# ELU in two ACT passes and one DVE pass, and a one-pass normalisation, in a linear-attention layer

## What is computed

```python
        qkv = x @ w_qkv + b_qkv
        ...
        q = jax.nn.elu(q) + 1.0
        k = jax.nn.elu(k) + 1.0
        kv = jnp.einsum('bhnd,bhne->bhde', k, v)
        out = jnp.einsum('bhnd,bhde->bhne', q, kv)
        z = 1.0 / (jnp.einsum('bhnd,bhd->bhn', q, k.sum(axis=2)) + 1e-08)
        out = out * z[..., None]
```

## Time and profile before

| | |
|---|---|
| device time, three runs | 1470.67, 1473.27, 1473.92 us (median 1473.27) |
| span of the profiled execution | 1432.3 us |
| device time of the profiled execution | not recorded by itself |
| the stage of the change | from 336 us (first transfers) to 492 us (last scatter) |
| busy: PE, DVE, ACT, POOL | 1099.4, 834.6, 544.6, 484.7 us |
| mean granted TensorE clock | 0.886 of full speed |

### The profile page before, as it was taken

One profiled execution on the slowest core, in us unless ns is written; L12 is line 12 of the kernel. 1 busy time (PEld: TensorE's weight loads), 2 busy tenths in 40 slices (PEclk: granted clock), 3 DMA queues, 4 the chain that ended last, 5 costly groups with the idle time before them and its releaser, 6 DMA issues.

```text
span 1432.3 us, 39482 instructions
## 1 busy us (share of the span) xinstructions
PE 1099.4 (77%) x16860; PEld 814.9 (57%) x16860; DVE 834.6 (58%) x2486; ACT 544.6 (38%) x919; POOL 484.7 (34%) x555
## 2 busy tenths in 40 slices
PE   5899938992766398376788888889888887762996
PEld 3677727992655266253455565656565564442885
DVE  6577744654877311525857768585858675733343
ACT  3223102221542132141456373737465553450442
POOL 3123331332767300424131324324231403022576
PEclk9999969996987599577899999999999999776998
DMA  9940033653200241211112021222121100103685
GB/s 375 397 180 18 19 112 105 198 160 114 89 15 23 62 95 47 66 51 52 50 45 61 12 69 52 56 58 63 51 62 48 46 22 11 53 20 102 150 212 112
DMA packets 89204, 126.46 MB, mean 88 GB/s; under 512 B 14914, under 2 KB 67396, under 8 KB 88612
## 3 DMA queue, kind: packets, MB, share of 16 engines
q1 hardware_dynamic: 72868, 107.79, 24.0%
q0 software_dynamic: 11936, 14.04, 4.4%
q10 hardware_dynamic: 4224, 2.10, 0.5%
HBM read 53.10 MB, written 44.83 MB: 68 GB/s over the span
## 4 chain that ended last, share of the span: by engine, by line
PE 26%; DVE 19%; ACT 8%; DMA 3%; POOL 3%; issue 3%; SPq 2%; POOLq 0%; DVEq 0%; ACTq 0%
DVE mx L1497 9%; ACT MW L1710 4%; PE ps L791 2%; PE ps L713 2%; PE ps L965 2%; PE ps L699 2%; PE ps L805 2%; DVE mx L1488 2%; PE ps L908 2%; PE ps L899 2%; PE ps L821 1%; PE ps L900 1%; DMA MW<-l_moe_dram 1%; DVE X L1028 1%; DVE bst L1000 1%
## 5 line engine op out<-in xcount | busy, mean ns | idle before, releaser
L1497 DVE TENSOR_REDUCE mx<-ps 128x2 f32<-128x1024 f32 (+3 forms) x176 | 188.5, 1120 | 33.2 <-PE ps L938 33.1
L1710 ACT ACTIVATE MW<-ps 128x1024 f32<-128x1024 f32 x160 | 154.6, 1028 | 74.9 <-PE ps L950 74.4
L1830 POOL DMA_INDIRECT xs<-xr,sidu x96 | 95.4, 994 | 141.9 <-DVE sidu L1158 104.2
L1773 POOL TENSOR_SCALAR rst<-bmv 128x4 f32<-128x4 f32 x64 | 15.6, 243 | 246.2 <-DVE bmv L1003 241.1
L713 PE MATMUL ps<-tmpA,MW 128*128 128x256 f32 x336 | 92.7, 392 | 6.9 <-DMA MW<-l_moe_dram 3.5
L965 PE MATMUL ps<-MW,Vp 128*16 128x128 f32 x2560 | 87.8, 279 | 3.6 <-ACT MW L1710 3.5
L531 PE MATMUL ps<-W,xr 128*128 128x128 f32 x192 | 38.3, 335 | 64.5 <-DVE xr L1013 35.3
L1858 POOL DMA_INDIRECT out_dram<-qf,toku x46 | 71.5, 1554 | 42.7 <-DVE toku L1320 34.5
L699 PE MATMUL ps<-MW 128*128 128x128 f32 x672 | 82.0, 275 | 3.0 <-DVE qf L1305 1.5
L699 PEld LDWEIGHTS ps<-MW 128*128 128x128 f32 x672 | 78.5, 192 | 3.4 <-issue 3.3
L938 PE MATMUL ps<-K,Q 64*128 64x512 bf16 (+3 forms) x512 | 62.8, 319 | 22.2 <-DVE mx L1497 15.3
(11 more groups left out here) (319 smaller groups left out, 2537.9 us busy)
## 6 DMA issues: line engine op xcount, KB each, us to landing
xs<-hb SPq DMA_DIRECT2D x66, 384.0 KB, 4.2
MW<-l_moe_dram SPq DMA_DIRECT2D x19, 768.0 KB, 5.5
MW<-l_moe_dram SPq DMA_DIRECT2D x23, 578.0 KB, 5.1
Q<-spl SPq DMA_DIRECT2D x48, 128.0 KB
K<-spl SPq DMA_DIRECT2D x48, 128.0 KB
Q<-spm SPq DMA_DIRECT2D x48, 128.0 KB
K<-spm SPq DMA_DIRECT2D x48, 128.0 KB
tmpA<-xs SPq DMA_DIRECT2D x42, 132.0 KB, 2.2
```

The source lines that it names most:

```text
L1497: V.tensor_reduce(out=mx[1][:, :, s0:s0 + ns, t], in_=p.rearrange("p (e n) -> p e n", e=2)[:, :, 0:ns * nk].rearrange("p e (s k) -> p e s ...
L1710: A.activation(P3[k % 2][:, 1024 * half:1024 * half + 1024], p, ACT.Exp).then_inc(drained[u], 1)
L1830: G.indirect_dma_start(out=xs[L], out_offset=bass.IndirectOffsetOnAxis(ap=sidu[:, 4 * b + t:4 * b + t + 1], axis=0), in_=src[:, t, 0:128 i ...
```

## The change

POOL no longer takes part in `l1_qe` and `l1_ke`, and neither does DVE. ACT writes Relu(-x), which is -min(x, 0), to `rr`, and then Exp of its negative in place. DVE's `l1_qf` and `l1_kf` become one operation, max(x, 0) + `rr`, in place over q or k. The due times of `l1_qe` and `l1_ke` on ACT change from 51.43 and 51.92 to 46.43 and 46.92. In `l1_o` one operation over all four tiles takes the place of four. Semaphores `q1_neg`, `k1_neg`, `q1_exp`, `k1_exp` take the place of `elu_min` and `elu_exp`.

```diff
--- before.py
+++ after.py
@@ -115,10 +115,10 @@
     ("l1a_y", dict(ACT=19.59, POOL=61.22)),
     ("l1a_n", dict(PE=52.57, ACT=31.47)),
     ("l1_q", dict(PE=66.51, ACT=45.57)),
-    ("l1_qe", dict(DVE=48.64, ACT=51.43, POOL=41.55)),
+    ("l1_qe", dict(ACT=46.43)),
     ("l1_kv", dict(PE=64.39, DVE=35.61)),
     ("l1_qf", dict(DVE=57.21)),
-    ("l1_ke", dict(DVE=43.88, ACT=51.92, POOL=44.94)),
+    ("l1_ke", dict(ACT=46.92)),
     ("l1_kf", dict(DVE=53.29)),
     ("l1_st", dict(PE=90.45, DVE=62.59)),
     ("l1_o", dict(PE=93.61, DVE=67.61)),
@@ -299,7 +299,7 @@
          "pv0", "pv1", "og_out0", "og_out1",
          "logits_on", "hot", "tsub", "texp", "slots", "scatter0", "scatter1", "y0_in", "y1_in", "mixed",
          "tab", "gx0", "gx1", "gx2", "gx3", "gw0", "gw1", "gw2", "gw3", "turned", "gT", "g_act", "g_down", "g_y", "g_tok",
-         "y_out0", "y_out1", "y_out2", "y_out3", "rope", "tanh", "padded", "elu_min", "elu_exp", "elu_max", "q1_in", "q1_on", "k1_on",
+         "y_out0", "y_out1", "y_out2", "y_out3", "rope", "tanh", "padded", "q1_neg", "k1_neg", "q1_exp", "k1_exp", "q1_in", "q1_on", "k1_on",
          "mx0", "mx1", "m_turn", "mT", "m_down", "m_out0", "m_out1", "m_y"]
         + [f"{n}{k}" for n in ("stats", "rstd", "xn_done") for k in range(4)]
         + [f"{n}{k}" for n in ("hi", "rest", "mid", "low", "max_hi", "max_mid", "max_low") for k in range(2)]
@@ -1355,16 +1355,10 @@
                     x_at[b] = (sem["mixed"], b + 1)
                 elif name == "l1a_s":
                     ln_stats((name, b))
-                elif name == "l1_qe":
-                    e.wait_ge(drained_of(("l1_q", b)), after(("l1_q", b)))
-                    if b > 0:
-                        e.wait_ge(sem["q1_on"], b)
-                    settled()
-                    own.end(V.tensor_scalar(out=kf[:, :], in0=q1[i], scalar1=0.0, scalar2=None, op0=ALU.max))
                 elif name == "l1_qf":
-                    e.wait_ge(sem["elu_exp"], 2 * b + 1)
-                    settled()
-                    V.tensor_tensor(out=q1[i], in0=rr[0][:, :], in1=kf[:, :], op=ALU.add).then_inc(sem["q1_on"], 1)
+                    e.wait_ge(sem["q1_exp"], b + 1)
+                    V.scalar_tensor_tensor(out=q1[i], in0=q1[i], scalar=0.0, in1=rr[0][:, :], op0=ALU.max,
+                                           op1=ALU.add).then_inc(sem["q1_on"], 1)
                 elif name == "l1_kv":
                     u, n, p = unit((name, b))
                     pv = p.rearrange("p (t n) -> p t n", t=4)
@@ -1375,15 +1369,9 @@
                     V.tensor_tensor(out=k1[i], in0=pv[:, :, 0:128], in1=bc(w("l1_bkv")[:, 0:128], 1, [128, 4, 128]), op=ALU.add)
                     V.tensor_tensor(out=l1v[i][:, :, 0:128], in0=pv[:, :, 128:256], in1=bc(w("l1_bkv")[:, 128:256], 1, [128, 4, 128]),
                                     op=ALU.add).then_inc(drained[u], 1)
-                elif name == "l1_ke":
-                    e.wait_ge(drained_of(("l1_kv", b)), after(("l1_kv", b)))
-                    if b > 0:
-                        e.wait_ge(sem["k1_on"], b)
-                    own.end(V.tensor_scalar(out=op_[0].rearrange("p g q -> p (g q)"), in0=kk, scalar1=0.0, scalar2=None, op0=ALU.max))
                 elif name == "l1_kf":
-                    e.wait_ge(sem["elu_exp"], 2 * b + 2)
-                    settled()
-                    V.tensor_tensor(out=kk, in0=rr[1][:, :], in1=op_[0].rearrange("p g q -> p (g q)"), op=ALU.add).then_inc(sem["k1_on"], 1)
+                    e.wait_ge(sem["k1_exp"], b + 1)
+                    V.scalar_tensor_tensor(out=kk, in0=kk, scalar=0.0, in1=rr[1][:, :], op0=ALU.max, op1=ALU.add).then_inc(sem["k1_on"], 1)
                 elif name == "l1_st":
                     u, n, p = unit((name, b))
                     if b > 3:
@@ -1404,10 +1392,8 @@
                     settled()
                     own.end(V.reciprocal(rd, rd))
                     settled()
-                    for t in range(4):
-                        m = V.tensor_tensor(out=tc4[:, t, :].rearrange("p (h e) -> p h e", h=H), in0=pv[:, t, 0:128].rearrange("p (h e) -> p h e", h=H),
-                                            in1=bc(rd[:, t, :], 2, [128, H, 8]), op=ALU.mult)
-                    m.then_inc(drained[u], 1)
+                    V.tensor_tensor(out=tc4[:, :, :].rearrange("p t (h e) -> p t h e", h=H), in0=pv[:, :, 0:128].rearrange("p t (h e) -> p t h e", h=H),
+                                    in1=bc(rd, 3, [128, 4, H, 8]), op=ALU.mult).then_inc(drained[u], 1)
                 elif name == "l1_pj":
                     x_at[b] = (sem["bias_done"], B + b + 1)
                     add_x4((name, b), b)
@@ -1635,8 +1621,13 @@
                     A.activation(q1[i], p[:, 0:512], ACT.Identity, bias=w("l1_bq")).then_inc(drained[u], 1)
                 elif name in ("l1_qe", "l1_ke"):
                     j = 0 if name == "l1_qe" else 1
-                    e.wait_ge(sem["elu_min"], 2 * b + j + 1)
-                    A.activation(rr[j][:, :], rr[j][:, :], ACT.Exp).then_inc(sem["elu_exp"], 1)
+                    src = q1[i] if j == 0 else k1[i].rearrange("p t d -> p (t d)")
+                    made = ("l1_q" if j == 0 else "l1_kv", b)
+                    e.wait_ge(drained_of(made), after(made))
+                    e.wait_ge(sem["q1_on" if j == 0 else "k1_on"], b)
+                    A.activation(rr[j][:, :], src, ACT.Relu, scale=-1.0).then_inc(sem["q1_neg" if j == 0 else "k1_neg"], 1)
+                    e.wait_ge(sem["q1_neg" if j == 0 else "k1_neg"], b + 1)
+                    A.activation(rr[j][:, :], rr[j][:, :], ACT.Exp, scale=-1.0).then_inc(sem["q1_exp" if j == 0 else "k1_exp"], 1)
                 elif name == "l1_tr":
                     u, n, p = unit((name, b))
                     if b > 0:
@@ -1872,15 +1863,6 @@
                     rstd((name, b))
                 elif name == "l1a_y":
                     add_bias(("l1a_n", b), "l1_bproj")
-                elif name == "l1_qe":
-                    e.wait_ge(drained_of(("l1_q", b)), after(("l1_q", b)))
-                    e.wait_ge(sem["q1_on"], b)
-                    G.tensor_scalar(out=rr[0][:, :], in0=q1[b % 4], scalar1=0.0, scalar2=None, op0=ALU.min).then_inc(sem["elu_min"], 1)
-                elif name == "l1_ke":
-                    e.wait_ge(drained_of(("l1_kv", b)), after(("l1_kv", b)))
-                    e.wait_ge(sem["k1_on"], b)
-                    G.tensor_scalar(out=rr[1][:, :], in0=k1[b % 4].rearrange("p t d -> p (t d)"), scalar1=0.0, scalar2=None,
-                                    op0=ALU.min).then_inc(sem["elu_min"], 1)
                 elif name == "l1t_x":
                     scatter(1, b)
             for k in range(2):
```

## The result

The changed kernel takes 1484.64 us in the median (11 runs, 1477.47 to 1490.01), the kernel before 1473.27 us (11 runs, 1467.06 to 1477.48) on the same chip: a ratio of 1.0078, interval 1.0059 to 1.0097. That is 11.4 us or 0.8% slower, where +6.0 us was forecast; the time lies inside the range of 1467 to 1488 us. The change is almost twice the forecast, and lies outside the 3 to 10 us that the forecast called its own mechanism.

A forecast was written before the change was run, and what follows sets the result against it. The prediction took a ring of handovers between engines in the linear-attention stage as the bound. Terms 3.0 + 3.5 + 0.8 + 3.5 - 3.3 - 1.3 - 0.2 gave +6.0 us: 1473.27 to 1479.3 us, range 1467 to 1488 us.

The forecast's parts named there:

- its own mechanism: Linear-attention stage: ACT's moved passes lengthen the handovers between engines, slower by 3 to 10 us, chance 0.49.
- The moved block ahead of `l1_tr`: On ACT, both Relu and Exp pairs now stand between XT and l1a_y, delaying l1_tr; about 2.4 us before next work.
- The wait for `l1_qf`: ACT's first Relu of a batch waits for DVE's l1_qf of the batch before, about 1 us in four or five batches.
- The length of the block: ACT from the end of l1_qf to l1_tr: 4.0 us with l1a_y; one Relu and Exp pair 1.30 us.
- DVE from `l1_kv` to the end of `l1_qf`: DVE's part of the four steps between batches 3 and 7, taken as 3.9, 5.4, 6.05 and 5.4 us.
- PE from `l1_pj` to the next `l1_kv`: PE's part of the four steps between batches 3 and 7, taken as 6.8, 6.8, 5.5 and 6.1 us.
- The clearly slower rival: PE's lower clock holds through l1_kv in each of four rounds, 7.2 us more: +13, 1486.5 us; chance 0.12.
- Before batch 3: Table load and first block ahead of l1a_y make l1_tr of batch 0 and l1_kv of batch 3 start 3.0 us later.
- After batch 7: From l1_kv of batch 7 to ACT's next normalisation: 16.2 us instead of 17.54, so -1.3 us.
- The relief of POOL and DVE: POOL loses 16 min passes, about 1.65 us each; DVE loses 16 clamps, those of l1_ke 0.42 to 0.83 us.
- the faster rival: ACT's block does not delay the handovers, leaving only POOL's and DVE's savings: -7.6 us, 1465.7 us; chance 0.19.
- The rule against Relu on ScalarE: Skill's rule that relu, max and min belong on VectorE; with the clamp there the sum would be about -0.5.

The follow-up runs named there:

- e1_late: Changed kernel with the due times of l1_qe and l1_ke on ACT put back, so both pairs stand behind l1_tr; ratio 0.9974 to the kernel before.
- e3_two_buffers: Changed kernel with two buffers for each rr, so a Relu waits for the addition of two batches earlier; ratio 1.0043 to the kernel before.
- e4_pool_min_fused: Kernel before with only DVE's maximum and addition fused, min staying on POOL and normalisation in four passes; ratio 0.9976 to the kernel before.
- e7_pool_min_norm: Kernel before with the fused DVE pass and one-pass normalisation, min staying on POOL, Exps at their old place; ratio 0.9980 to the kernel before.
- e8_pool_min_early: Kernel before with fused DVE pass, one-pass normalisation and Exps moved ahead of l1_tr, min staying on POOL; ratio 1.0101 to the kernel before.
- e9_both_behind_fn: Changed kernel with two rr buffers, both pairs behind l1_tr and the q pair also behind l1f_n's XT copy; ratio 0.9977 to the kernel before.
- e11_late_fill: Changed kernel with two rr buffers, both pairs behind l1_tr, and one unread matmul filling PE's pause there; ratio 0.9947 to the kernel before.
- e6_after_again: Changed kernel, unaltered, run on the other sort of chip; ratio 1.0055 to the kernel before on that chip.

## Why the prediction was right, and where its size was off

- **The moved block ahead of `l1_tr`: right, and shown.** It was named as the part that counts, and `e1_late` takes it back alone.
- **The wait for `l1_qf`: right.** Forecast about 1 us in four or five batches; measured 0.81 to 1.69 us in six, batch 6 among them, which the prediction had thought free of it. `e3_two_buffers` puts it at 4.9 us of the four steps and 3.2 us of the stage.
- **The length of the block: right.** Forecast 4.0 us from the first Relu to `l1_tr`, measured 3.92, and 2.38 where forecast was 2.45 for batch 6; a pair 1.30, measured 0.66 + 0.63. The Trainium skill, page "ScalarE: Activation LUTs", section "What ACT_TABLE_LOAD costs", gives 186 ns + 0.833 ns per element for an ACTIVATE with immediate scale and bias: 0.61 us here, an estimate by that page; the rows agree with 0.61 to 0.64. No table load was added.
- **DVE from `l1_kv` to the end of `l1_qf`: right in sum, two rounds off.** Forecast 3.9, 5.4, 6.05, 5.4; to the Relu's start they are 4.9, 5.5, 5.5 and 5.5. The 1.0 us in the first is the fused pass of 1.58 us in place of 0.68 (below). The fusion had been costed at nothing for each pass, which holds for 15 of the 16. With the block, `l1_kv` to `l1_pj` was forecast at 37.6 us over the four and is 37.9.
- **PE from `l1_pj` to the next `l1_kv`: the term that was mis-sized.** The sum took 6.8, 6.8, 5.5 and 6.1; measured are 9.57, 6.69, 6.87 and 7.70, together 30.8 instead of 25.2. That is 5.6 us, nearly all of the 6.0 by which the steps (68.78) exceed the forecast's (62.8). I had taken two stretches of the kernel before, 6.8 and 5.5, and their mean as if they held for all rounds, though its own four are 6.8, 9.5, 5.5 and 7.4, together 29.1: the 3.76 us of `l1_kv` in the earlier trace rows stand in the 9.5. So 3.9 of the 5.6 us were there before the change and had been dropped from the sum without a reason, and 1.7 were added by it. The clearly slower rival had the mechanism, the lower clock after PE's pause, as an addition of 7.2 us; what was wrong was to hold it for an alternative to the forecast, since both act in the same round. It had the lower level hold through `l1_kv` in all four rounds; it did in one (3.53 us, 1.97 in the others). Its +13 us is nearer to the measured +11.4 than the forecast's +6.0, and it had been given 0.12.
- **Before batch 3:** +3.0 forecast; `l1_kv` of 3 starts 37.4 us into the stage instead of 35.4, so +2.0.
- **After batch 7:** 16.2 forecast, 15.56 measured (467.66 to 452.10, the start of the next normalisation on ACT), where it was 17.54 before. To the end of the stage only 0.9 us of that gain is left, where 1.3 + 0.2 had been forecast.
- **The relief of POOL and DVE: smaller than in the faster rival.** That rival had 7.6 us. Where the passes stand behind `l1_tr` the stage is shorter than before by 3.8 (`e1_late`), 4.6 (`e4_pool_min_fused`) and 1.4 us (`e7_pool_min_norm`), and none of the three ratios excludes no change. The old step 6 to 7, of which 3.3 us were to go with POOL's passes, gave back 1.7.
- **The rule against Relu on ScalarE** (the Trainium skill, "ScalarE: Activation LUTs", "Rules for kernel authors"): a clamp on VectorE in the same place was not run. `e1_late` shows that the passes cost nothing measurable on ACT where ACT is waiting anyway, and `e8_pool_min_early` that having them elsewhere, there on POOL, doesn't help where the place is wrong.
- **The sentence on 41.0 us around the span was wrong**, as the first section shows. It changed no term, since the sum was one of differences inside the stage.

## What to carry to other kernels

Where each engine works a fixed list in order, cost a moved instruction by who waits for the instruction behind it, not by its length: 2.5 us of work a batch, and the wait that came with it, ahead of the copy that PE waits for cost some 15 us over eight batches, and the same work behind it nothing that could be measured. Add up every round of the kernel before, the slow ones too, before taking a good one for all. When a change lengthens a pause of TensorE, take the matmuls right behind the pause at the lower clock unless a row of this very round says otherwise; here a few matmuls whose result nobody reads kept it high. Before adding a difference to a median, see that the span and the median are of the same chip.

## What the hardware showed that I had not expected

**The clock after a pause.** The granted clock has two levels, 1.2 and 2.4 GHz, and `l1_pj` shows which one holds: 1.16 us at the upper, about 2.08 at the lower. After pauses of 6.03, 5.52, 5.52 and 3.98 us (changed kernel) it took 2.07 or 2.08 each time. After the shorter ones it goes either way: 1.16 after 1.43 and 1.97 us in the kernel before and after 3.35 us in `e7_pool_min_norm`, but 2.08 after 1.83 us in `e9_both_behind_fn`, and after only 0.68 us in the kernel before (429.88 us):

```profile
412.90 2.08 PE L771 MATMUL ps<-W,oT 128*128 128x128 f32 x8 [1.83 <-ACT oT L1638]
...
425.52 1.16 PE L771 MATMUL ps<-W,oT 128*128 128x128 f32 x8 [0.68 <-ACT oT L1638]
```

So the length of the last pause alone doesn't tell; what does was not settled. The Trainium skill, page "TensorE: Matmul & The Clock Gate", section "HAM oscillation — how this bites in real kernels", describes a kernel that falls back to the lower clock at each wait before a tile and starts every tile cold; this trace agrees, in that `l1_pj` is at the lower clock after each of the four pauses named, and the four stretches have 0.52, 0.76, 0.74 and 0.65.

**A DVE pass held up by one of POOL.** POOL's timeline of the changed kernel at the place where the fused pass took 1.58 us (386.57 to 388.15):

```profile
386.00 1.60 POOL L1778 TENSOR_TENSOR X<-X,W 128x512 f32<-128x512 f32 x1
```

It takes 1.60 us where other passes of that line take 1.10. A DVE pass of the same form (L1374, 385.97 to 386.65) had begun just before it; POOL's took 0.5 us more, and the DVE pass behind it, begun in the meantime, ends 0.55 us after POOL's. The source view of L1360 gives the length for all of one buffer, shortest, middle and longest in ns:

```profile
L1360 DVE SCALAR_TENSOR_TENSOR Vp<-Vp,rr x4: 681/682/1583, 386.6 to 470.2; 128x512 f32<-128x512 f32 x4
```

In most other runs with fused passes one or two of the 16 are long, up to 1.60 us; in `e8_pool_min_early` and `e11_late_fill` none is. The Trainium skill, page "SBUF — State Buffer", section "Who interferes with whom", says that a DVE pass with two inputs in SBUF and a GpSimd pass that reads SBUF exclude each other for a whole instruction, first come first served; these rows agree, with 0.9 us lost once. The fusion did not bring this: in the kernel before the median of the unfused additions is 0.68 to 0.69 us, but one (L1386, 450.91 us) took 1.97, overlapping the same kind of pass on POOL (L1787, 451.22 to 452.32).

**The chips.** The kernel before differs by 2.5% between two chips (1434.75 and 1469.89 us), and the changed kernel by under 0.5 us in this stage. The traces part in the long stages of layers 2 and 3: from the third batch on, the steps of `l2_q` take about 80 us in the trace of before and mostly 85 to 88 us in that of after, but 77 to 79 us for the same changed kernel in `e6_after_again`, so this is the chip and not the change. Why it is so was not followed.
